# Fused four-layer program: bf16 zero operands in the feed-forward stages, and eight-slot preparation with a per-head softmax on ScalarE in the mixed attention

## The reference, cut to what matters

```python
qs = softmax(q, axis=-1); ks = softmax(k, axis=-1)      # over the 128 features
gl = log_sigmoid(k) / 16                                # gate, cumulated over time
# linear attention: S = S * exp(gl) + ks^T v ; o_gla = qs S
sq, sk = rotary(q), rotary(k)                           # ordinary causal attention
y = softmax(causal(sq sk^T * 128**-0.5)) v
o = (0.5 * y + 0.5 * o_gla) @ Wo
```

## Time and profile before

| | |
|---|---|
| median of 3 runs | 3144.28 us |
| profiled execution, its own time | 3143.49 us |
| its span | 3141.6 us |
| busy in the span | TensorE 76%, its weight loads 59%, VectorE 55%, ScalarE 39%, GpSimd 30% |
| mean granted TensorE clock | 0.869 of 2.4 GHz |
| mixed attention | about 799 to 1757 us |
| dense feed-forward stages | about 670 to 777, 1758 to 1937, 3023 to 3133 us |

### The profile page before, as it was taken

How to read it: one execution, slowest core, us unless ns; L and a number is a source line. 1 busy time by engine, 2 the same in 40 slices (tenths; PEclk the granted TensorE clock), 3 DMA queues, 4 the chain that set the end, 5 groups by cost and what they waited for, 6 DMA issues and landing times. The chain is left out here.

```text
span 3141.6 us, 40049 instructions
## 1 busy us (share of the span) xinstructions
PE 2401.7 (76%) x11600; PEld 1850.7 (59%) x11600; DVE 1742.7 (55%) x4172; ACT 1240.2 (39%) x3558; POOL 929.7 (30%) x1053
## 2 busy tenths in 40 slices
PE   3699999987477887788877897355996126999787
PEld 2577766654256666666666675254885015777665
DVE  3677742234277777777777423554333377777333
ACT  1355543320344543454544312155574104555321
POOL 0366620034123322333233000062003403555234
PEclk7899999987689999999999988577998558999888
DMA  4300013332100000000000010061253200000343
GB/s 196 154 27 27 27 59 93 93 95 86 72 1 1 1 1 1 1 1 1 1 1 1 30 41 24 2 251 37 89 161 120 65 0 28 10 2 1 128 152 117
DMA packets 95439, 172.36 MB, mean 55 GB/s; under 512 B 17874, under 2 KB 73134, under 8 KB 93624
## 3 DMA queue, kind: packets, MB, share of 16 engines
q1 hardware_dynamic: 76856, 126.47, 11.9%
q0 software_dynamic: 18432, 44.05, 4.4%
HBM read 111.76 MB, written 65.01 MB: 56 GB/s over the span
## 5 line engine op out<-in xcount | busy, mean ns | idle before, releaser
L1222 POOL TENSOR_TENSOR a_s<-a_s,a_rinv 128x128 f32<-128x128 f32 (+1 forms) x512 | 243.4, 505 | 256.5 <-DVE a_rinv L1398 252.2
L1349 ACT ACTIVATE a_s<-a_s,a_nmax 128x128 f32<-128x128 f32 (+1 forms) x512 | 227.7, 446 | 179.1 <-DVE a_nmax L1392 174.3
L1790 POOL TENSOR_TENSOR a_rcos<-a_qk,a_cos 128x1280 f32<-128x1280 f32 x32 | 92.6, 2895 | 667.2 <-ACT a_qk L1967 667.2
L851 POOL DMA_INDIRECT f_yg<-y,l_slot x128 | 126.3, 987 | 406.7 <-issue 364.8
L211 POOL DMA_INDIRECT xg<-all_xn,l_slot_d x192 | 194.3, 1012 | 39.3 <-issue 39.3
L2063 DVE SCALAR_TENSOR_TENSOR a_s<-a_pS,all_cmask 128x384 f32<-128x384 f32 x128 | 70.9, 554 | 214.1 <-PE a_pS L1874 214.1
L605 DVE TENSOR_TENSOR e_hid<-e_gate,e_pG 128x128 f32<-128x128 f32 (+1 forms) x192 | 59.4, 309 | 234.2 <-ACT e_gate L580 234.2
L1288 PE MATMUL a_pv<-a_pT,a_v 128*128 128x256 f32 x512 | 161.0, 396 | 18.0 <-ACT a_pT L1359 18.0
L1392 DVE TENSOR_REDUCE a_nmax<-a_s 128x1 f32<-128x128 f32 (+1 forms) x512 | 156.7, 348 | 8.8
L1268 PE MATMUL a_ring<-a_kT,a_qT 128*128 128x256 f32 x512 | 160.3, 396 | 0.0
L1863 PE MATMUL a_pq<-all_ident,a_src 128*128 128x128 f32 x640 | 111.5, 316 | 55.2 <-DVE a_tt L2090 42.5
(11 more groups left out here) (290 smaller groups left out, 6666.2 us busy)
## 6 DMA issues: line engine op xcount, KB each, us to landing
e_xs<-xg SPq DMA_DIRECT2D x176, 128.0 KB, 2.2
y<-e_ys SPq DMA_DIRECT2D x176, 128.0 KB, 1.7
l_wres<-in_L_resident SPq DMA_DIRECT2D x3, 4224.0 KB
xg<-blank_zeros SPq DMA_DIRECT2D x4, 3072.0 KB
s_w<-in_L_bank SPq DMA_DIRECT2D x32, 384.0 KB, 4.0
l0e_wres<-in_L_resident SPq DMA_DIRECT2D x4, 2432.0 KB
f_w<-in_L_bank SPq DMA_DIRECT2D x16, 448.0 KB, 3.2
f_w<-in_L_shared SPq DMA_DIRECT2D x14, 448.0 KB, 3.5
```

The costliest lines, as they stand in the source:

```text
L851: nc.gpsimd.indirect_dma_start(out=yg[i % GR][:, :], out_offset=None, in_=y, in_offset=bass.IndirectOffsetOnAxis(ap=slot[:, t, j:j + 1], a ...
L1222: last = nc.gpsimd.tensor_tensor(rows, rows, rinv[:, h, t:t + 1].broadcast_to([P, hi - lo]), ALU.mult)
L1349: last = nc.scalar.activation(s[:, h % SLOTS, lo:hi], s[:, h % SLOTS, lo:hi], ACT.Exp, bias=nmax[:, h % SLOTS, t:t + 1], accum_out=rsum[:, ...
```

## The change

It has two parts. The operand `zero` becomes bfloat16, for both of its matmuls; all its values are zero, and nothing else in `gated_ffn` changes.

In `attention_mixed` the preparation of a group is spread over eight slots instead of four, so two groups are under way at any time, and `LEAD` goes from 6 to 10. The two halves of the projection share one bank `pq` in phases 0 and 1; the turned blocks get one bank `pt`, in phases 5 (m = 0), 6 (m = 1, 2) and 7 (m = 3, 4); the value projection is in phase 2, `sums` and `decay_qk` in phase 4. The value tiles go from three to four. The feature softmax changes its form: VectorE takes the negated maxima of each token tile (phases 1 and 2), the subtraction and the sum over `e` are gone, and ScalarE computes ten exponentials of 128 features each, five for each token tile (phases 2 and 3), with the negated maximum as bias and the sum as accumulated output.

```diff
-        zero = sp.sb("zero", [1, 512])
+        zero = sp.sb("zero", [1, 512], BF16)
...
-    LEAD = 6
+    LEAD = 10
...
-        pq = [sp.ps(f"pq{i}", [P, 512]) for i in range(2)]
+        pq = sp.ps("pq", [P, 512])
+        pt = sp.ps("pt", [P, 512])
...
                 for n in range(NG):
-                    pool.wait_ge(qk_ready, n + 1)
+                    pool.wait_ge(q_read, QT * (n + 1))
...
-                    after(pool, tt_done, NTT * n)
+                    after(pool, tt_done, NTT * (n - 1) + 3 if n else 0)
...
                 def project(n, t):
-                    after(pe, tt_even_read, 3 * n)
-                    after(pe, tt_odd_read, 2 * n)
+                    after(pe, q_read, QT * n + t)
...
                 def turn(n, m):
-                    if m == 3:
-                        pe.wait_ge(tt_odd_read, 2 * n + 1)
-                    if m == 4:
-                        pe.wait_ge(tt_even_read, 3 * n + 2)
+                    if m % 2:
+                        pe.wait_ge(tt_even_read, 3 * n + (m + 1) // 2)
+                    else:
+                        after(pe, tt_even_read if m == 0 else tt_odd_read, 3 * n if m == 0 else 2 * n + m // 2)
...
                 for slot in SLOTS_ALL:                                   # TensorE
+                    at = [group_at(slot, phase) for phase in range(8)]
                     scores(slot + 2)
-                    project(fresh, 0); turn(turning, 0); turn(turning, 1)
+                    project(at[0], 0) / project(at[1], 1)
+                    turn(at[6], 1) / turn(at[7], 3)
                     output(slot - 2)
-                    project(fresh, 1)
                     (project_keys | decays)
                     turn_p(slot)
-                    project_values(fresh); turn(turning, 2); turn(turning, 3)
+                    project_values(at[2]) / turn(at[5], 0)
                     values(slot - 1)
-                    turn(turning, 4)
+                    turn(at[6], 2) / turn(at[7], 4)
...
-                def softmax_exps(n):                                     # ScalarE
-                    act.wait_ge(sub_ready, n + 1)
-                    nc.scalar.activation(e[:, :, :, :], e[:, :, :, :], ACT.Exp).then_inc(e_ready, 1)
+                def softmax_exps(n, t):
+                    act.wait_ge(top_ready, QT * n + t + 1)
+                    for h in range(HB):
+                        at = t * HB + h
+                        last = nc.scalar.activation(e[:, t, h, :], qk[:, t, h, :], ACT.Exp, bias=top[:, at:at + 1],
+                                                    accum_out=total[:, at:at + 1])
+                    last.then_inc(e_ready, 1)
...
                 # ScalarE: exps, softmax_exps(at[2], 0) / (at[3], 1), gather_qk(at[0], 0) / (at[1], 1), gates,
                 #   copy_p, copy_values(at[2]), copy_turned(at[5], 0), copy_o, copy_turned(at[6], 2) / (at[7], 4)
...
-                def shift(n):                                            # VectorE
-                    nc.vector.tensor_reduce(top[:, :], qk[:, :, :, :].rearrange(nf), AX_X, ALU.max).then_inc(top_ready, 1)
-                    dve.wait_ge(top_ready, n + 1)
-                    nc.vector.tensor_tensor(e[...], qk[...], top[...] broadcast, ALU.subtract).then_inc(sub_ready, 1)
+                def tops(n, t):
+                    dve.wait_ge(q_read, QT * n + t + 1)
+                    after(dve, e_ready, QT * n)
+                    nc.vector.tensor_reduce(top[:, t * HB:(t + 1) * HB], qk[:, t, :, :], AX_X, ALU.max,
+                                            negate=True).then_inc(top_ready, 1)
                 def sums(n):
-                    nc.vector.tensor_reduce(total[:, :], e[:, :, :, :].rearrange(nf), AX_X, ALU.add).then_inc(total_ready, 1)
                     nc.vector.reciprocal(inv[n % 2][:, :], total[:, :]).then_inc(inv_ready, 1)
...
                 # VectorE: maxima, copy_turned(at[6], 1) / (at[7], 3), join, tops(at[1], 0) / (at[2], 1),
                 #   sums(at[4]) and decay_qk(at[4]), add_out
```

More of the change, by code:

```diff
@@ L1698, in attention_mixed @@
         down = [sp.sb(f"down{i}", [P, QT, HKV, EH]) for i in range(2)]
-        v = [sp.sb(f"v{i}", [P, QT, EH]) for i in range(3)]
+        v = [sp.sb(f"v{i}", [P, QT, EH]) for i in range(4)]
         top = sp.sb("top", [P, QT * HB])
@@ L1907, in _ @@
                 for slot in SLOTS_ALL:
-                    fresh, turning = group_at(slot, 0), group_at(slot, 3)
+                    at = [group_at(slot, phase) for phase in range(8)]
                     if 0 <= slot + 2 < NH:
                         scores(slot + 2)
-                    if fresh is not None:
-                        project(fresh, 0)
-                    if turning is not None:
-                        turn(turning, 0)
-                        turn(turning, 1)
+                    for phase in range(2):
+                        if at[phase] is not None:
+                            project(at[phase], phase)
+                    if at[6] is not None:
+                        turn(at[6], 1)
+                    if at[7] is not None:
+                        turn(at[7], 3)
                     if 0 <= slot - 2 < NH:
                         output(slot - 2)
-                    if fresh is not None:
-                        project(fresh, 1)
                     for phase in range(4):
@@ L1925, in _ @@
                         turn_p(slot)
[L1926 to L1930 removed]
+                    if at[2] is not None:
+                        project_values(at[2])
+                    if at[5] is not None:
+                        turn(at[5], 0)
                     if 0 <= slot - 1 < NH:
                         values(slot - 1)
[L1933 to L1934 removed]
+                    if at[6] is not None:
+                        turn(at[6], 2)
+                    if at[7] is not None:
+                        turn(at[7], 4)
             @block.scalar
@@ L2002, in _ @@
                 for slot in SLOTS_ALL:
-                    fresh, summing, turning = group_at(slot, 0), group_at(slot, 2), group_at(slot, 3)
+                    at = [group_at(slot, phase) for phase in range(8)]
                     if 0 <= slot + 1 < NH:
                         exps(slot + 1)
-                    if summing is not None:
-                        softmax_exps(summing)
-                    if fresh is not None:
-                        gather_qk(fresh)
-                    if turning is not None:
-                        copy_turned(turning, 0)
+                    for t in range(QT):
+                        if at[2 + t] is not None:
+                            softmax_exps(at[2 + t], t)
+                    for phase in range(2):
+                        if at[phase] is not None:
+                            gather_qk(at[phase], phase)
                     for phase in range(4):
@@ L2101, in _ @@
                 for slot in SLOTS_ALL:
-                    shifting, summing, turning = group_at(slot, 1), group_at(slot, 2), group_at(slot, 3)
+                    at = [group_at(slot, phase) for phase in range(8)]
                     if 0 <= slot + 2 < NH:
                         maxima(slot + 2)
-                    if turning is not None:
-                        copy_turned(turning, 1)
+                    if at[6] is not None:
+                        copy_turned(at[6], 1)
+                    if at[7] is not None:
+                        copy_turned(at[7], 3)
                     if 0 <= slot + 1 < NH:
                         join(slot + 1)
-                    if shifting is not None:
-                        shift(shifting)
-                    if summing is not None:
-                        sums(summing)
-                        decay_qk(summing)
-                    if turning is not None:
-                        copy_turned(turning, 3)
+                    if at[1] is not None:
+                        tops(at[1], 0)
+                    if at[2] is not None:
+                        tops(at[2], 1)
+                    if at[4] is not None:
+                        sums(at[4])
+                        decay_qk(at[4])
                     if 0 <= slot - 5 < NH and slot % GQ == 1:
```

66 lines of the change are left out of this document (27 added, 39 removed).

## The result

The changed kernel takes 2921.53 us in the median of 4 runs (2916.85 to 2925.24), against 3145.66 for the kernel before on the same chip: a ratio of 0.9287, 95% interval 0.9268 to 0.9306, faster. The forecast was 2947, and the range 2895 to 3020 holds the time. The profiled execution took 2925.2 us, its span is 2923.5.

A forecast was written before the change was run, and what follows sets the result against it. No single engine was taken to bound the mixed attention, only lumps laid on each in turn. From 3143.5 us, -148 for the attention and -49 for the zero products gave 2946.5, taken as 2947, range 2895 to 3020.

The forecast's parts named there:

- The bound: Mixed attention: no engine fills the 27.8 us period, which sums lumps on each in turn; TensorE's own work is 19.3 us.
- The slots: TensorE's time in the four slots A to D of an attention period: 4.9, 5.3, 4.95 and 5.4, period 20.5 us.
- The second blocked join: Attention: VectorE's join in slot D also held by GpSimd's rotation; half of 1.6 us in each of 30 groups, +24 us.
- The sum for the attention: Mixed attention: -163 for the periods, +24 for a blocked join, +4 at the start, -13 at the end: -148 us.
- The sequence groups: Attention, one group in four makes a sequence's keys, gates and decays: 10.8 us more than a plain period, 31.3 us.
- The engines: Work for an attention group: VectorE 16.9 us plus a blocked join or two, ScalarE 16.0 us, exponentials 0.38 us apart.
- The zero products: Openings and closings in the dense stages get cheaper in bf16: first halves 12.8, second halves 16.0, closings 20.4, together -49 us.
- Rival 1: Attention: the stalls only move and a period settles at 23.5 to 24 us, giving 3046 us, or 2997 with half; chance 0.24.
- Rival 2: Dense stages: the clock follows busyness, whatever the product, so half of the openings' 28.8 us is lost, 2961 us; chance 0.09.
- Rivals 3 and 5: bf16 zeros cost as much as float32, 2996 us, chance 0.03; the eight attention slots run as long as before, 3095, 0.04.
- rival 4: Attention: ScalarE's lumps hold copies so TensorE stalls in slots C and D; at a 30 us period 3160 us; chance 0.03.
- the clock adds nothing: Attention: clock rises from 0.94 to 1.0 only where the 3.46 us stalls go; no extra gain, as work was priced at full clock.

The follow-up runs named there:

- e11: The changed kernel with the two sine products of GpSimd's rotation left out, so the output lacks the sine terms; 2912.2 us, ratio 0.9257.
- e4: The changed kernel with GpSimd's first rotation product done twice, 2.9 us more for each group; 3010.6 us, ratio 0.9580 to the kernel before.
- e5: The changed kernel with each of the ten feature exponentials done twice, 3.8 us more ScalarE work a group; 3077.8 us, ratio 0.9778 to the kernel before.
- e2: The changed kernel (eight slots, bf16 zeros) with the softmax in its old form, one exponential and VectorE's subtraction and sum; 3049.3 us, ratio 0.9681.
- e3: The kernel before (four slots, float32 zeros) with only the softmax in the new form of ten exponentials; 3091.2 us, ratio 0.9814.
- e10: The changed kernel with one more exponential per token half, 0.77 us more ScalarE work a group; 2936.5 us, ratio 0.9333 to the kernel before.

## Why the prediction was right, and what was mis-sized

**The bound.** Right. The prediction said that the 27.8 us were lumps laid end to end and that spreading leaves TensorE's own 19.3 us of work; the loop now runs at 19.4 busy of 20.1.

**The slots.** Forecast 4.9, 5.3, 4.95 and 5.4; measured 4.97, 5.31, 4.93 and 4.89. Three are right to 0.1 us. D is 0.5 too dear: I made VectorE's copy of turned blocks 3 late by 0.6 through the blocked join of C. In the timeline that copy starts at 1396.26, right behind D's masks, and turn 4 follows at 1397.23 without a wait; C's join had been over 2.5 us before the copy, so its 0.9 us were absorbed. e11 shows the same from the other side: without that block the period does not move.

**The second blocked join, +24 us, is the term that failed.** It did not happen. I put the end of the rotation on D's join. In fact GpSimd's addition ends at 1396.85 and D's join starts at 1397.05, 0.2 us later. There was another place for a second block that I did not see, in C itself. The addition has a wait of its own in the changed order (0.72 us), for the group before's turn 2, whose blocks it overwrites; C's join ends at 1393.76, in the gap that this wait leaves, and the addition starts at 1393.94. The diff showed that wait; I read it as a guard that is long met and did not ask where it puts the addition. What the gap is worth shows in e4: it puts 2.9 us of GpSimd's work there, C's join is blocked a second time, and a group pays 3.3 us. No run takes the wait itself away.

**The sum for the attention.** Forecast -148, measured -172.1. The last 30 distances went from 854 to 680.5 us, -173.5, where the forecast had -163 + 24 = -139: 24 from the join that did not come, some 6 from the periods in step (D cheaper, the sequence's groups a little dearer), and 4 from the first two of these distances, 13.5 and 23.2 us, in which the slots are not yet full. Start and end together were +1.4 us, where I had +4 - 13 = -9: the tail behind the last rotation start is 6 us longer than before, not shorter, and the start is 5 us shorter, not 4 longer. So the two largest misses, 34 us too little gain in the loop and 10 too much at its ends, had opposite signs; they leave 24 of the 25 us by which the forecast was too high.

**The sequence groups.** Right: 30.1 + 1.7 in the group before are 31.8, the forecast 31.3, and by the mechanism named. In the timeline TensorE waits for ScalarE's copy behind the logarithm and its table loads, then for the decay exponentials behind the five of the softmax; the windows row is the stretch behind it:

```profile
1343.32 0.66 PE L1859 MATMUL a_pt<-all_ident,a_src 128*128 128x128 f32 x4 [1.68 <-ACT a_tt L1983]
...
1348.87 2.04 PE L1843 MATMUL a_pkd<-a_wv,all_xT 128*128 128x128 f32 x8 [2.84 <-ACT a_down L1954]
```

```profile
1349.00:1352.00 3.00, 3.00 (x13) 2.82 (x14) 0.00 (x0) 0.49 (x2) 0.00 (x0) 0.53 0.00 0
```

**The engines.** VectorE has 16.6 us of a plain period, forecast 16.9 and a blocked join or two; ScalarE 14.1, and 15.8 with the sequences' share, forecast 16.0; ten exponentials 0.38 us apart, as forecast.

**The zero products.** -50.6 against -49. One-pass products took 0.43 and 0.22 us, the value taken from the nearest row. First halves 12.9 (12.8), closings 20.5 (20.4), second halves 19.2 (16.0); the excess is the clock, which stayed up behind two of three closings. These parts are read at other points than the stages and add up to 52.6.

**The rivals.** Rival 1 (the stalls only move, 0.24) did not happen; e5 shows that with twice the exponentials it does. Rival 2 (the clock follows busyness) is not refuted as a mechanism: in the first half of layer 0 the real products ran at half clock for 6.0 us where it had been 3.6, which took back 0.9 of the 4.3 us; over the six openings it was outweighed. By the Trainium skill's page "TensorE: Matmul & The Clock Gate", section "What's actually happening", busyness releases the clock; e2, e4 and e5, where the half clock stands behind each long stall, agree with it, and this, not the openings, is where it mattered. The rule alone does not price a stall: e3 had six of 1.9 us and five of 2.6 in the loop in step and the clock fell behind three of these eleven, e10 six of 3.2 and one. Rivals 3 and 5 fell with the 1.86 us and the 20.1 us, rival 4 with both slots C and D under 5 us.

**What the prediction missed though its number held.** It said that the clock adds nothing. In the kernel before each 3.46 us stall was followed by 3.0 us at 0.53, so every removed stall paid some 1.4 us more than its length. I had it only because I added up the new period from work at full clock. The other way round, it had no reason why a half-done change should gain so little: by its sum the period of e2 would have been near VectorE's 20.8 us, and it was 26.5. Part of e3's small gain was the clock's as well, by the estimate under e3. What stays open is why the clock falls behind some stalls and not behind others of the same length; no run here varies that alone.

## What to carry to other kernels

When several engines hand work round in a fixed order, add up each slot on each engine; a period comes down to the busiest engine's work only when no slot holds a lump longer than that engine's own work there, and removing one of two lumps gains little (52 and 63 us alone, 179 together). A stall of TensorE is priced with the slow stretch that can follow it, and the trace has to say whether it does; a wait that a change adds to one engine is also a change of the time at which that engine's work collides with another's. Work that comes rarely, such as a logarithm with its two table loads, belongs in the slot where its engine waits anyway: here that was worth 57 us more, 2864 against 2921.

## What the runs showed of the hardware

- The granted clock fell to half (0.50 to 0.54) around or just behind TensorE stalls of 3.46 us (before), 3.22 (e2), 1.89 with 0.69 soon after (e4), 1.94 and 2.90 (e5) and 2.84 (the changed kernel's sequence groups), each time, and came back within 3 to 7 us. Behind the 0.7 us wait of each plain period, and the 1.1 of e10, it stayed at 1.00.
- The length of one stall does not decide it: in the loop in step it stayed up behind five of six stalls of 1.9 us and three of five of 2.6 us in e3, and behind five of six of 3.2 us in e10.
- A VectorE operation with two SBUF operands is held by a GpSimd instruction that runs beside it, each for itself: the join's two took 0.75 us free, 1.64 with the first held (the changed kernel), 4.35 with both held (e4).
- Ten exponentials of 128 features cost 3.8 us of ScalarE, 0.39 each and 0.19 for the read of the running sum, which overlaps with the next by half; one of 1280 costs 1.27.
- Products ahead of an opening raised the clock for the zero products (1.03 us for four instead of 1.86), and it fell again to 0.54 within 5 us, behind a wait of 1.39.
